# A graph layer in one kernel: the last sort level cut short and turned, four buffers for x, two loads moved into stage two, twelve joint pairs, and the value matrix from split parts

## The reference, cut to what matters

```python
xn = layernorm(x)                                   # rows of 512
h  = relu(xn @ W1 + b1) @ W2 + b2                   # 512 -> 256 -> 512
x1 = x + h + segment_sum(h[dst], src) + mix(xn)
# mix: h = layernorm(xn); k, q, v = split(h @ kqv_w + kqv_b)
#      kp = exp(k @ w.T - |k|^2/2)/16; qp likewise from q    (256 features)
#      kptv = v^T kp                                  (512 x 256)
#      y = qp @ kptv^T / (qp . sum(kp)); y = v + y @ proj_w + proj_b
#      return y + gelu(layernorm(y) @ mlp_w1 + b) @ mlp_w2 + b
out = x1 + wavelet_ffn(layernorm(x1))               # halves of a row, fc1 256, fc2
```

## Time and profile before

| | us |
|---|---|
| runs | 1723.69, 1730.77, 1717.75 (median 1723.69) |
| profiled execution, its own time | 1722.76 |
| its span | 1720.9 |
| busy: PE, DVE, ACT, POOL | 1535.3, 1152.4, 821.4, 996.6 |

### The profile page before, as it was taken

The page is one execution under the profiler, slowest core; times in us unless marked ns, Lnnn a source line. Parts: engine busy times, 40 slices in busy tenths (PEclk is TensorE's granted clock), DMA queues, the critical chain, the costliest instruction groups (busy, mean ns, idle before and its releaser), DMA issues.

```text
span 1720.9 us, 27109 instructions
## 1 busy us (share of the span) xinstructions
PE 1535.3 (89%) x8983; PEld 1269.8 (74%) x8983; DVE 1152.4 (67%) x2550; ACT 821.4 (48%) x1896; POOL 996.6 (58%) x1057
## 2 busy tenths in 40 slices
PE   5999999998888899999999977998898897788996
PEld 3778877777657788888888866876777786466664
DVE  6899999998344566756665663655554563478786
ACT  2234444444364444444544474665566462355552
POOL 3024444333677766767777777777777774556610
PEclk9999999999999999999999998999999998799998
DMA  6023232322335655556556566555555553566642
GB/s 198 13 68 119 90 93 84 102 75 90 111 104 157 196 164 165 171 174 205 179 173 185 170 193 203 194 189 189 187 190 190 185 181 119 171 204 206 200 164 76
DMA packets 88683, 263.65 MB, mean 153 GB/s; under 512 B 18555, under 2 KB 20603, under 8 KB 88546
## 3 DMA queue, kind: packets, MB, share of 16 engines
q1 hardware_dynamic: 47490, 149.05, 25.5%
q0 software_dynamic: 41056, 112.88, 23.0%
HBM read 210.64 MB, written 44.90 MB: 148 GB/s over the span
## 4 chain that ended last, share of the span: by engine, by line
PE 36%; DMA 27%; DVE 19%; ACT 7%; issue 6%; POOL 3%; SPq 1%; DVEq 1%; POOLq 0%; ACTq 0%
DMA z_rows<-sb_step 7%; DMA sb_step<-x 7%; DVE sb_weights L1573 6%; DMA sb_step<-sb_acc 4%; DMA sb_step<-x_t 3%; ACT sb_weights L1381 3%; PE bank L996 3%; PE bank L998 3%; PE bank L997 3%; DMA z_rows<-sb_weights 2%; DMA sb_weights<-x 2%; PE bank L788 1%; PE bank L790 1%; PE bank L789 1%; PE bank L1035 1%
## 5 line engine op out<-in xcount | busy, mean ns | idle before, releaser
L683 POOL DMA_INDIRECT sb_weights<-hidden_rows,sb_weights x830 | 825.2, 994 | 343.2 <-issue 220.0
L1381 ACT ACTIVATE sb_weights<-sb_const,sb_weights 128x125 f16<-128x125 f16 x880 | 266.1, 388 | 39.5 <-PE turn_bank L949 39.5
L1880 DVE TENSOR_TENSOR sb_acc<-sb_acc,bank 125x257 f32 x220 | 92.8, 422 | 191.1 <-PE bank L949 172.2
L1573 DVE TENSOR_TENSOR sb_weights<-sb_weights 128x512 f32<-128x512 f32 (+3 forms) x256 | 164.4, 684 | 3.6
L1880 DVE TENSOR_TENSOR sb_acc<-sb_acc,turn_bank 125x257 f32 x220 | 92.4, 420 | 109.0 <-PE turn_bank L949 99.6
L650 POOL TENSOR_SCALAR sb_const<-sb_const 125x2 f32<-125x2 f32 x25 | 9.6, 385 | 239.2 <-ACT sb_step L1283 239.2
L1299 ACT ACTIVATE sb_step<-sb_step 125x256 f32<-125x256 f32 x100 | 48.0, 503 | 202.6 <-DVE sb_step L1746 201.8
L788 PE MATMUL bank<-sb_w_parts,sb_x_high 128*125 128x512 f32 (+1 forms) x400 | 139.3, 348 | 0.0
L790 PE MATMUL bank<-sb_w_parts,sb_x_low 128*125 128x512 f32 (+1 forms) x400 | 135.2, 338 | 0.0
L789 PE MATMUL bank<-sb_w_parts,sb_x_high 128*125 128x512 f32 (+1 forms) x400 | 135.0, 337 | 0.0
L1385 ACT ACTIVATE sb_weights<-sb_weights,sb_const 128x1000 f16<-128x1000 f16 x110 | 124.2, 1129 | 3.6
(11 more groups left out here) (374 smaller groups left out, 4366.7 us busy)
## 6 DMA issues: line engine op xcount, KB each, us to landing
sb_step<-x SPq DMA_DIRECT2D x55, 500.0 KB
sb_step<-x_t SPq DMA_DIRECT2D x50, 500.0 KB, 6.9
sb_weights<-hidden_rows,sb_weights POOLq DMA_INDIRECT x830, 4.4
y_rows<-sb_step SPq DMA_DIRECT2D x25, 500.0 KB
sb_weights<-x SPq DMA_DIRECT2D x20, 500.0 KB
sb_step<-y_rows SPq DMA_DIRECT2D x17, 500.0 KB
z_rows<-sb_step SPq DMA_DIRECT2D x17, 500.0 KB
sb_step<-z_rows SPq DMA_DIRECT2D x13, 504.0 KB
```

Of the source, the lines that this page charges most:

```text
L683: pool.indirect_dma_start(out=ring[:, r % RING * 2 + h, 0:HID], out_offset=None, in_=table, in_offset=bass.IndirectOffsetOnAxis(ap=row_of[ ...
L1381: mm = act.activation(hit[q % 2][:, i, :], iota_h[:, :], ACT.Abs, bias=less_lane[:, q * BP + i // 2, i % 2:i % 2 + 1])
L1573: sort_op(dve.tensor_tensor(half(target, c, lo), a, b, op))
L1880: dve.tensor_tensor(dst, dst, (BE, BH)[n % 2][0:P, 0:RW], ALU.add).then_inc(g_add, 1)
```

## The change

- `SORT` ends at (17, 8): the last eight stages are gone, and `turn_keys(len(SORT))` turns the keys a last time. The rank parts read them from `turn_bank` in PSUM, and the last key of each block is a maximum (`tensor_reduce`) over 256. Instead of VectorE's copy (L1600), ScalarE copies the half of the turned keys (`lower_keys`, semaphore `keys_ok`). `SORT_DEAL` and `TURNED_LATE` change, two rank parts move a step forward.
- `hk` is split into a part rounded to fp32r and a remainder, and the value matrix is three fp32r products (high x high, high x low, low x high) for each of 16 tiles.
- z and x get a fourth buffer, `z_first[0]`. `late_io(a)` now waits for z(a-2) first, then loads x(a+2), then y(a+3), then stores z(a-1); x(3) is loaded after `pe_fc1`. `load_yd(2)` and the second MLP matrix are issued in stage two, in step 23, behind a wait on that step's last product.
- `JOIN` goes from 6 to 12. `LAST`, which takes the rest of the 440 pairs, goes from 52 to 46.

The diff, cut to its core; the same change of `% 3` to `% 4` in `load_xd`, `skip_rows` and the last MLP rows is left out:

```diff
--- before
+++ after
@@ -33,12 +33,12 @@
-SORT = [(level, bit) for level in range(1, 18) for bit in reversed(range(level))]
+SORT = [(level, bit) for level in range(1, 18) for bit in reversed(range(level)) if level < 17 or bit >= 8]
-    return sum((4 if bit == level - 1 and level < 17 else 2) + turned(k) for k, (level, bit) in enumerate(SORT[:i]))
+    return sum(4 if bit == level - 1 and level < 17 else 2 for level, bit in SORT[:i])
@@ -56,9 +56,9 @@
 SORT_DEAL = ((15, 1), (5, 3), (2, 6), (3, 3), (2, 3), (6, 1), (4, 0), (7, 0), (3, 2), (5, 2), (5, 1),
-             (2, 5), (4, 3), (2, 3), (2, 3), (3, 2), (2, 5), (9, 0), (3, 4), (1, 4), (3, 2), (3, 4))
+             (2, 5), (4, 3), (2, 3), (2, 3), (3, 2), (2, 5), (6, 0), (3, 3), (4, 3), (6, 0), (0, 0))
 SORTED = len(SORT_DEAL)
-TURNED_LATE = (6, 11, 12, 13, 15, 16, 17, 19, 20, 21)
+TURNED_LATE = (19,)
@@ -76,12 +76,35 @@
+def turned_part(part):
+
+    if part < len(SORT_PARTS) and SORT_PARTS[part][0] < SORT_PARTS[part][1] and turned(SORT_PARTS[part][0]):
+        return SORT_PARTS[part][0]
+
+
+def turns_before(i):
+
+    return sum(turned(k) for k in range(i))
+
+
+def low_span(i):
+
+    level, bit = SORT[i]
+    across = level >= 10 and bit >= 7
+    return 2 ** bit if not across else 2 ** (bit - 10) if bit >= 10 else 128 * 2 ** (bit - 7)
+
+
+def span_half(v, c, lo):
+
+    return v.rearrange("p (h c l) -> p h c l", c=2, l=lo)[:, :, c]
+
+
 def spread(count, parts):
-TURN, SECOND, BETWEEN, MLP, JOIN, TAIL_TURN = (6, 14, 16), [14, 10, 9, 8] + [7] * (STEPS - 4), 4, [10] + [6] * (STEPS - 1), 6, 2
+TURN, SECOND, BETWEEN, MLP, JOIN, TAIL_TURN = (6, 14, 16), [14, 10, 9, 8] + [7] * (STEPS - 4), 4, [10] + [6] * (STEPS - 1), 12, 2
 BEFORE_SECOND = [sum(TURN) + sum(SECOND[:u]) for u in range(STEPS + 1)]
@@ -321,7 +344,9 @@
-        hk, kptv = x_in[:, 0].rearrange("p a (b c) -> p (a b) c", c=M), x_in[:, 1].rearrange("p a (b c) -> p (a b) c", c=M)
+        kptv = x_in[:, 1].rearrange("p a (b c) -> p (a b) c", c=M)
+        hk_high = [W2_HIGH[:, k * M:(k + 1) * M] for k in range(KC)]
+        hk_low = [G_HIGH[:, k * M:(k + 1) * M] for k in range(3)] + [W2_HIGH[:, KC * M:(KC + 1) * M]]
@@ -342,7 +367,7 @@
         y3 = [halves[1].rearrange("p (a b) -> p a b", b=D), y3_odd, z_first[1]]
-        z3 = [x3[:, 0], x3[:, 1], z_first[2]]
+        z3 = [x3[:, 0], x3[:, 1], z_first[2], z_first[0]]
@@ -387,14 +412,15 @@
         x_ld, x2_ld, xt_ld = (pair(n) for n in ("x_in", "x2_in", "xT_in"))
-        x3_ld, y_ld, z_st = ([sem(f"{n}{k}") for k in range(3)] for n in ("x3_in", "y_in", "z_stored"))
+        y_ld = [sem(f"y_in{k}") for k in range(3)]
+        x3_ld, z_st = ([sem(f"{n}{k}") for k in range(4)] for n in ("x3_in", "z_stored"))
         acc_ld = pair("sums_in")
         st_sum, st_mean, st_sq, scaled = (sem(n) for n in ("stat_sums", "stat_means", "stat_squares", "row_scales"))
-        sort_ok, sort_tr = sem("sort_exchanges"), sem("keys_transposed")
+        sort_ok, sort_tr, keys_ok = sem("sort_exchanges"), sem("keys_transposed"), sem("lower_keys_copied")
@@ -501,6 +527,9 @@
                     load_yd(0)
+                    sp.wait_ge(w_mm, 4 * STEPS + 1)
+                    load_yd(2)
+                    sp.dma_start(mlp2_w, chunks(d["L0_mix_mlp_w2"])).then_inc(w2m_in, 16)
                 if t.u < STEPS - 1:
@@ -549,19 +578,22 @@
                 sp.wait_ge(z_ok, t.u + 2)
-                sp.dma_start(z_d[1:P + 1, t.u * 2:t.u * 2 + 2, :], z3[t.u % 3][0:P]).then_inc(z_st[t.u % 3], 16)
+                sp.dma_start(z_d[1:P + 1, t.u * 2:t.u * 2 + 2, :], z3[t.u % 4][0:P]).then_inc(z_st[t.u % 4], 16)
             def z_stored(t):
-                sp.wait_ge(z_st[t.u % 3], 16 * (t.u // 3 + 1) + 1)
+                sp.wait_ge(z_st[t.u % 4], 16 * (t.u // 4 + 1) + 1)
             def late_io(a):
+                if 2 <= a and a + 2 < STEPS:
+                    z_stored(steps[a - 2])
+                    load_xd(a + 2)
                 if a + 3 < STEPS:
                     load_yd(a + 3)
-                if 2 <= a and a + 1 < STEPS:
-                    z_stored(steps[a - 2])
-                    load_xd(a + 1)
+                if a == TAIL_TURN:
+                    sp.wait_ge(ev("pe_fc1"), 1)
+                    load_xd(3)
                 if a == STEPS - 2:
@@ -577,8 +609,6 @@
             load_xd(0)
-            sp.dma_start(mlp2_w, chunks(d["L0_mix_mlp_w2"])).then_inc(w2m_in, 16)
-            load_yd(2)
             load_xd(1)
@@ -591,7 +621,7 @@
             sp.wait_ge(late_in, 5 * 16 + 1)
-            for t in steps[-3:]:
+            for t in steps[-4:]:
                 z_stored(t)
@@ -837,8 +867,10 @@
-                if part < len(SORT_PARTS) and SORT_PARTS[part][0] < SORT_PARTS[part][1] and turned(SORT_PARTS[part][0]):
-                    turn_keys(SORT_PARTS[part][0])
+                if part == 2 * (SORTED - 1):
+                    turn_keys(len(SORT))
+                elif turned_part(part) is not None:
+                    turn_keys(turned_part(part))
@@ -1048,9 +1080,10 @@
                 for k in range(KC):
-                    for h in (0, 1):
-                        pe.matmul(bk, w2_values[h][:, k, c * 128:(c + 1) * 128], hk[:, k, :],
-                                  start=k == 0 and h == 0, stop=False)
+                    high, low = (w2_values[h][:, k, c * 128:(c + 1) * 128].bitcast(F32R) for h in (0, 1))
+                    pe.matmul(bk, high, hk_high[k].bitcast(F32R), start=k == 0, stop=False)
+                    pe.matmul(bk, high, hk_low[k].bitcast(F32R), start=False, stop=False)
+                    pe.matmul(bk, low, hk_high[k].bitcast(F32R), start=False, stop=False)
                 mm = pe.matmul(bk, bv_bc[0:1, c * 128:(c + 1) * 128], ks_bc[0:1, :], start=False, stop=True)
@@ -1346,10 +1379,18 @@
                 act.activation(parted_h[t.b][0:P, :, 0:HID], rt[0:P], ACT.Relu).then_inc(r_high, 1)
+
+            def lower_keys(part):
+
+                i = turned_part(part)
+                if i is not None:
+                    act.wait_ge(sort_tr, turns_before(i) + 2)
+                    act.copy(span_half(keys[i % 2], 0, low_span(i)), span_half(turn_bank[:, :], 0, low_span(i))).then_inc(keys_ok, 1)
             for t in each_step(1):
                 act.wait_ge(scaled, t.u + 2)
+                lower_keys(2 * t.u)
                 if t.u == STEPS - 1:
@@ -1362,6 +1403,7 @@
                     stats(next_step(t))
+                lower_keys(2 * t.u + 1)
                 q_kept(t.u)
@@ -1496,11 +1538,11 @@
             copy_accT(steps[1])
-            hits_until(BEFORE_LAST - JOIN)
+            hits_until(BEFORE_LAST - JOIN + spread(JOIN, 3)[0])
             for u in range(3):
                 copy_degrees(steps[u])
-                if u == 1:
-                    hits_until(BEFORE_LAST)
+                if u < 2:
+                    hits_until(BEFORE_LAST - (spread(JOIN, 3)[2], 0)[u])
             for b in range(STEPS):
@@ -1590,15 +1630,13 @@
                 level, bit = SORT[i]
-                across = level >= 10 and bit >= 7
-                lo = 2 ** bit if not across else 2 ** (bit - 10) if bit >= 10 else 128 * 2 ** (bit - 7)
+                lo = low_span(i)
                 dve.wait_ge(sort_ok, sort_n[0] + 1)
                 if turned(i):
-                    dve.wait_ge(sort_tr, (level - 10) * 2 + (bit == 6) + 2)
+                    dve.wait_ge(sort_tr, turns_before(i) + 2)
+                    dve.wait_ge(keys_ok, turns_before(i) + 2)
                     b_at = turn_bank[:, :]
-                    sort_op(dve.tensor_copy(half(a_at, 0, lo), half(b_at, 0, lo)))
-                    dve.wait_ge(sort_ok, sort_n[0] + 1)
                 if bit < level - 1:
@@ -1615,7 +1653,7 @@
-            sorted_keys = keys[len(SORT) % 2]
+            sorted_keys = turn_bank[:, :]
@@ -1760,9 +1798,9 @@
                 if u == SORTED:
-                    dve.wait_ge(sort_ok, sort_n[0] + 1)
-                    last_keys = sorted_keys.bitcast(I32).rearrange("p (q c) -> p q c", c=256)[:, :, 255]
-                    ts(last_bits, last_keys, SRC_BITS + 7, ALU.logical_shift_right)
+                    dve.wait_ge(sort_tr, turns_before(len(SORT)) + 2)
+                    seq(dve.tensor_reduce(last_keys, sorted_keys.rearrange("p (q c) -> p q c", c=256), AXIS.X, ALU.max))
+                    ts(last_bits, last_keys.bitcast(I32), SRC_BITS + 7, ALU.logical_shift_right)
                     ts(last_tile, last_bits, float(KEY_BASE), ALU.subtract)
@@ -1849,15 +1887,15 @@
                 sort_part(2 * t.u)
-                if t.u == SORTED:
-                    rank_part(SORTED + 1)
+                if t.u in (SORTED - 1, SORTED):
+                    rank_part(t.u + 1)
                 dve.wait_ge(ex, t.g * 2 + 3)
                 q_and_v(t.u)
-                if SORTED <= t.u + 1 < STEPS:
-                    rank_part((SORTED, SORTED + 2, SORTED + 3)[t.u + 1 - SORTED])
+                if SORTED <= t.u < STEPS - 1:
```

(19 more changed lines are left out.)

## The result

| | before | after |
|---|---|---|
| median, us | 1725.05 (1717.75 to 1730.77, 4 runs) | 1749.2 (1747.86 to 1756.01, 4 runs) |
| ratio | | 1.0129, 95% interval 1.0092 to 1.0167 |
| span of the profiled execution, us | 1720.9 | 1747.6 |

The change is slower by 24 us. The forecast was 1718, its range ended at 1742. Stage one and the turn gained nearly what was forecast; stage three lost far more.

The account below looks back on a forecast made before the run. Bounds: VectorE, then TensorE, in stage one; five full DMA engines in stage three. Sort -13.5, value matrix -7, stage three +7, POOL's queue +11, fewer later pairs -3: -5.5 on 1722.76, forecast 1718 after median adjustment, range 1693 to 1742.

Parts of the forecast that it names:

- part 3: Stage three: five DMA engines full, waiting on z's landing empties the queue, 0.73 us a period, +13 over 18 periods.
- the +7: Stage three in all: start -4, queue gap +13, stage end -7, twelve joint pairs +5; bounds -9 to +30.
- Rival A: Stage three: the queue gap costs nothing, the period stays 16.57, 13 us less, 1705; chance 0.17.
- Rival B: Stage three: not bound by five engines; TensorE's step or POOL's gathers (15.1) decide, 26 less again, 1679; chance 0.08.
- Stage one: Shorter sort, with copies moved from VectorE to ScalarE: -13.5 us, bounds -7 and -22.
- Rival D: Stage one: ScalarE's copies come late in each of 15 turns, 8 of the 13.5 lost, 1726; chance 0.09.
- E: Joint: the change of JOIN does not delay roots(1), since something else holds step one, 1707; chance 0.06.
- Value matrix: Turn: fp32r products take 9.6 us against 18.8, VectorE's copies and subtractions add 1.7; net -7, bounds -3 and -9.
- Stage two and the start: Start of stage three: y(2) and the second MLP matrix issued some 10 us sooner, gain put at 4.
- End of stage three: Last three periods: no x load left to wait for, -7; twelve joint pairs delay z_ok(24), +5.
- roots(1): POOL's queue: 12 more gathers, 15.1 us, ahead of this root delay stage four; taken as +11, bounds +5 and +15.
- C: Stage three: the wait on the landing in late_io costs 2.0 us a period, +36 instead of +13, 1741; chance 0.17.

Follow-up runs that it names:

- y ahead of the wait: Changed kernel with only y(a+3) issued before SP's wait for the landing of z(a-2) in stage three: 1730.4 us, ratio 1.0007.
- the order alone: Kernel before with only SP's list reordered: wait for z(a-2), x(a+1), then y(a+3), three x buffers kept: 1762.7 us, ratio 1.0200.
- six pairs: Changed kernel with JOIN set from 12 back to 6: 1733.2 us, ratio 1.0021.
- Spreading the gathers: Changed kernel, twelve joint pairs, POOL six units behind at roots(1) and one unit less with each step: 1743.3 us, ratio 1.0081.
- the kernel with the old order: Kernel before plus only the new sort and value matrix, with three x buffers, old load order, six joint pairs: 1710.4 us, ratio 0.9872.

## Why the prediction was wrong

**The step that failed** is in part 3: "I take 0.73, by the nearer row: 18 periods, +13." In the trace a period grew by 18.37 - 16.57 = 1.80 us, +32.3, 19 more than taken. Not all of it is the dry queue. With y ahead of the wait, 1.07 a period (19.3) and 19 to 21 us of the whole time came back; the order alone, in the kernel before, cost 1.59 a period (28.6) and 35 us of the whole time. So the dry queue's price was 1.1 to 1.6 a period, one and a half to two times the 0.73. What the other 0.2 to 0.7 are stays open: both traces with four buffers and y ahead have periods over the old one (17.30 and 17.53), and the sum has no term for that. The mechanism and its place were right, the term was mis-sized. The nearer row misled: that a lone store's 6.16 against 5.52 compares a transfer on idle engines with one that shares them, so that the faster transfer hides most of the overhead, is argued, not shown; 6.16 against the 4.2 of a transfer at the engines' full rate was nearer to what was measured. Queue 0 didn't make up for the hole: it took 38.5% of 16 engines there and 25.3% in the hole of the order alone, against 33.2% over 1093 to 1406. The bounds of stage three have a slip, too: without the gap's 13 the +7 becomes -6, not -9. Rival A (the gap costs nothing) is refuted by the order alone, +35 us.

Of the 31.8 us between the last two columns of the table, 2.8 stand where the value products end, 8.7 come up to z(3), 19.3 in the 18 periods, -3.7 at the end of stage three, 3.9 up to roots(1) and 0.8 behind it.

**Rival B**, that stage three isn't bound by five engines, is refuted: spreading the same bytes over more engines gave the period 15.7, near the 15.1 that was put down for POOL's gathers. By the Trainium skill, "DMA: Bandwidth & Descriptors", section "Why a DMA increments its semaphore by 16 and not by 1", 112 rows go over 16 engines and 13 over 13; the runs agree in the time, from 1749 to 1688, and in the 84.7% of 16 engines' time at the last z store; how many engines each part had is in no row.

**Stage one**: -11.1 where the value products begin (437.15 for 448.28), forecast -13.5 + 1.7 = -11.8. ScalarE's copies took 0.59 each, and VectorE waited for them 8.8 us in all; TensorE's 97% is what is next. Right. One trace doesn't give it to a microsecond: in the 16 traces with the new sort the products begin at 435.7 to 439.9, in the three with the old sort and the old products at 448.3 to 451.9.

Rival D, little from the sort, is refuted by it, and E by roots(1).

**Value matrix**: -6.6 on TensorE (18.8 to 12.2) where -9.2 was forecast, since half of the products ran at clock 0.50 and the forecast had only the first group slow; VectorE's +1.6 (3.3 us from the sums to the first product, 1.7 before) was forecast. Mis-sized by 2.6, and this with luck: 15 of the 17 traces ran 36 or 48 products slow, which makes it 14 to 16 us for the 12.2 here. Alone on the kernel before it was worth 4 us, not 7, with all of them at 0.50; that the longer pause ahead of the products makes the low clock is argued, not shown, since the same pause stood before 12 slow products and before 48.

**Stage two and the start**: 4.7 of 17.7 us were given back by z(3), where 4 more had been forecast; the moved loads bought nothing that the whole times show. The y stores show it happen in stage two (from -17.7 to -12.8 at step 23); what gave it back was not settled.

**End of stage three** -5.7 (forecast -2 with the joint's +5, which six pairs confirm at 5.3). **roots(1)** +14.8 for the 15.1 of twelve gathers, of which the forecast took 11; with six fewer pairs stage four won back 2.2 in all, where 3 were forecast. Spreading the gathers won 10.5 from roots(0) on in the traces, near the 11, but 6 to 8 in the whole time. **Chances**: slower by over 1% had 0.17, and what stood against C, gathers in the gap, was argued and not priced.

## What to carry to other kernels

Where the engines of a queue are the bound, a wait on a landing ahead of the next issue costs time in every period, here 1.1 to 1.6 us on 16.6; keep one transfer queued behind it. Where a DMA share is far from full but transfers queue, look at how many engines one transfer uses: 112 + 13 rows instead of 125 took 3.7% off the changed kernel (ratio 0.9759 against 1.0129) and 1.9% off the kernel with the old order (0.9688 against 0.9872), and the fourth buffer nothing that was measured. Work postponed on an in-order queue moves the wait to its next consumer; deal it out over the steps that have slack.

## What the runs showed of the hardware

- Around a landing that SP waited for, queue 1 moved almost nothing for 2.0 us (1111.0 to 1113.0), and SP's issue at 1112.15 lies in the middle.
- The last z store (500 KB) took 30.2% of 16 engines' time over 4 us as one transfer of 125 rows, and 84.7% over 2 us as 112 and 13 rows, with 0.43 MB in both windows.
- After a pause of 3.32 us, TensorE's granted clock was at the lower level (0.50) for 12, 24, 36 or all 48 of the same products, in 17 traces; before, with a pause of 1.74, it was 0.60 over the first 4 us and then 0.98.
- On one chip the same program took 1853.6 us instead of 1726 to 1729, with stage one unchanged in the four traces taken there.
